# Experts' first layer as one fp32 matmul of 64 rows per tile, on alternating row halves of TensorE, in a MetaFormer block

## The reference, cut to what matters

```
xf = layernorm(t)                               # 2048 tokens x 64
logits = xf @ Wg + bg                           # 8 experts
top_w, top_i = top_k(logits, 2); top_w = softmax(top_w)
for e in range(8):                              # dense: every expert for every token
    h = gelu(xf @ W1[e] + b1[e])                # 64 -> 256, exact gelu
    out = out + w[:, e:e+1] * (h @ W2[e] + b2[e])   # 256 -> 64
t = t + out
```

## Time and profile before

| | |
|---|---|
| time of the profiled execution | 122.68 us |
| span from first to last instruction | 121.0 us |
| median of the three timed runs | 123.15 us |
| PE (matmul) busy | 116.2 us, 96% |
| DVE (VectorE) busy | 78.8 us, 65% |
| ACT (ScalarE) busy | 70.1 us, 58% |
| POOL (GpSimd) busy | 33.4 us, 28% |
| granted TensorE clock | 1.000 |

### The profile page before, as it was taken

The page is one execution under the profiler, slowest core; times in us unless marked ns, Lnnn a source line. Parts: engine busy times, 40 slices in busy tenths (PEclk is TensorE's granted clock), DMA queues, the critical chain, the costliest instruction groups (busy, mean ns, idle before and its releaser), DMA issues.

```text
span 121.0 us, 3332 instructions
## 1 busy us (share of the span) xinstructions
PE 116.2 (96%) x1282; PEld 86.3 (71%) x1282; DVE 78.8 (65%) x267; ACT 70.1 (58%) x134; POOL 33.4 (28%) x51
## 2 busy tenths in 40 slices
PE   6999999999999889999999999999999999999991
PEld 5589956777798688977766876766766667666660
DVE  0489595753868998988991089976409055096972
ACT  4338799030596255378892894591973929729200
POOL 6727999990000003033250031000000000000370
PEclk9999999999999999999999999999999999999999
DMA  3579600000000000000000059921099590001001
GB/s 105 176 169 215 176 8 0 5 5 5 0 0 5 0 3 0 0 5 0 0 0 3 11 158 232 240 69 43 11 242 225 197 241 11 0 0 54 1 0 46
DMA packets 5460, 8.05 MB, mean 67 GB/s; under 512 B 1412, under 2 KB 3908, under 8 KB 5444
## 3 DMA queue, kind: packets, MB, share of 16 engines
q1 hardware_dynamic: 5344, 7.80, 25.0%
q10 hardware_dynamic: 100, 0.03, 0.2%
HBM read 7.24 MB, written 0.59 MB: 65 GB/s over the span
## 4 chain that ended last, share of the span: by engine, by line
PE 83%; DVE 9%; ACT 2%; issue 2%; POOL 1%; POOLq 1%; DVEq 0%
PE PS L996 36%; PE PS L1293 18%; PE PS L1112 13%; PE PS L1071 2%; DVE HEADWISE L898 2%; PE PS L1178 2%; PE PS L1081 2%; PE PS L1008 2%; PE PS L1217 1%; PE PS L1094 1%; PE PS L1203 1%; POOL XP L449 1%; PE PS L1024 1%; DVE XB L717 1%; PE PS L1248 1%
## 5 line engine op out<-in xcount | busy, mean ns | idle before, releaser
L573 ACT ACTIVATE MS<-PS,B 128x512 f32<-128x512 f32 x48 | 29.1, 689 | 7.2 <-PE PS L996 7.0
L996 PE MATMUL PS<-XS,W1H 128*128 128x512 f32 x64 | 26.5, 414 | 0.0
L996 PE MATMUL PS<-XS,W1L 128*128 128x512 f32 x64 | 25.3, 395 | 0.0
L1293 PE MATMUL PS<-MS,W 128*64 128x256 f32 x192 | 22.3, 383 | 0.0
L874 DVE SCALAR_TENSOR_TENSOR WY<-PS,B,HEADWISE 128x256 f32<-128x256 f32 x24 | 10.5, 480 | 14.8 <-PE PS L1293 14.5
L1293 PEld LDWEIGHTS PS<-MS,W 128*64 128x64 f32 x192 | 13.2, 137 | 8.5 <-ACT MS L573 1.5
L1112 PE MATMUL PS<-HEADWISE,BANDS 32*32 32x448 f32 (+2 forms) x480 | 15.9, 564 | 0.0
L996 PEld LDWEIGHTS PS<-XS,W1H 128*128 128x128 f32 x64 | 12.0, 188 | 4.8 <-ACT MS L573 1.0
L449 POOL TENSOR_TENSOR XP<-XP,WY 128x256 f32<-128x256 f32 x4 | 3.2, 808 | 41.1 <-DVE WY L924 40.8
L1112 PEld LDWEIGHTS PS<-HEADWISE,BANDS 32*32 32x32 f32 x480 | 10.9, 103 | 4.5 <-issue 1.2
L996 PEld LDWEIGHTS PS<-XS,W1L 128*128 128x128 f32 x64 | 12.0, 188 | 1.8
(11 more groups left out here) (135 smaller groups left out, 182.6 us busy)
## 6 DMA issues: line engine op xcount, KB each, us to landing
HEADWISE<-spread_dram SPq DMA_DIRECT2D x14, 256.0 KB, 4.9
W<-in_w_dram SPq DMA_DIRECT2D x3, 512.0 KB, 7.9
X<-in_x_dram SPq DMA_DIRECT2D x2, 256.0 KB, 3.1
HEADWISE<-spread_dram SPq DMA_DIRECT2D x4, 128.0 KB, 3.1
out_dram<-XP SPq DMA_DIRECT2D x4, 128.0 KB, 2.6
W<-spread_dram SPq DMA_DIRECT2D x2, 256.0 KB, 5.3
VEC<-in_vectors_dram SPq DMA_DIRECT2D x1, 132.0 KB
WQ<-in_w_qkv_dram SPq DMA_DIRECT2D x2, 48.0 KB, 2.8
```

The costliest lines, as they stand in the source:

```text
L573: act.activation(hidden(n), PS[:, h_bank(n), :], ACT.Gelu, bias=B1[:, k:k + 1]).then_inc(gelu_done, 1)
L996: return pe.matmul(PS[0:parts, bank, cols[0]:cols[1]], lhsT, rhs, start=start, stop=stop)
L1293: i = pe.matmul(PS[C * b:C * b + C, bank, at:end], W2[:, KC * e + k, :], hidden(KC * (E * s + e) + k)[:, N * b:N * b + N], start=begins an ...
```

## The change

- W1 is used as it is, in fp32. `split_high` and `split_low`, `W1H`, `W1L` and `WGS` go; ScalarE only preloads the gelu table at that place.
- `scale` writes the same 64 normalised channels twice in one operation of 128 x 512; `low` goes. XS therefore holds the tokens twice, on rows 0 to 63 and on rows 64 to 127, as fp32.
- A hidden tile is one fp32 matmul over 64 rows: even tiles on the lower row half, odd tiles on the upper.
- The gate is one fp32 matmul over 64 rows per 128 tokens, with 8 columns; `read_gates` is one operation.
- `WH` has memory of its own, and its DMA and TensorE's first layers don't wait for the split.
- In the convolution the loops over r and c change places: r is the inner one, and all four `conv_ready` rise at the last four matmuls.

```diff
-        WGS = sb("WGS", [128, 2, E], F32R)
-        W1H, W1L = sb("W1H", [128, E * HID], F32R), sb("W1L", [128, E * HID], F32R)
+        WH = sb("WH", [128, KC, PT])
...
-            split_high()
+            act.preload_act_table(ACT.Gelu)
...
-            dve.wait_ge(w_high, 2)
-            split_low(0)
-            split_low(1)
-            dve.tensor_tensor(WGS[:, 1, :], WG[:, :], WGS[:, 0, :].bitcast(F32), ALU.subtract).then_inc(w_low, 1)
...
-                dve.tensor_tensor(XHL[:, s % 2, :, 0, :].bitcast(F32R), XC2[:, s % 2],
-                                  SM[:, s, 1, :].unsqueeze(2).broadcast_to([128, TILES, C]), ALU.mult).then_inc(hi_ready, 1)
-
-            def low(s):
-                dve.wait_ge(hi_ready, s + 1)
-                for t in range(TILES):
-                    i = dve.scalar_tensor_tensor(out=XHL[:, s % 2, t, 1, :].bitcast(F32R), in0=XC2[:, s % 2, t],
-                                                 scalar=SM[:, s, 1, t:t + 1], in1=XHL[:, s % 2, t, 0, :],
-                                                 op0=ALU.mult, op1=ALU.subtract)
-                i.then_inc(xh_ready, 1)
+                shape = [128, TILES, 2, C]
+                dve.tensor_tensor(XHL[:, s % 2], XC2[:, s % 2].unsqueeze(2).broadcast_to(shape),
+                                  SM[:, s, 1, :].unsqueeze(2).unsqueeze(2).broadcast_to(shape), ALU.mult).then_inc(xh_ready, 1)
...
                 for m in range(2, len(taps)):
-                    for r in range(4):
-                        for c in range(4):
+                    for c in range(4):
+                        for r in range(4):
                             i = tap(0, r, c, 2 - c // 2, c % 2, *taps[m], False, m == len(taps) - 1)
-                        if m == len(taps) - 1:
-                            i.then_inc(conv_ready, 1)
+                            if c == 3 and m == len(taps) - 1:
+                                i.then_inc(conv_ready, 1)
...
-                pe.wait_ge(w_low, 3)
+                pe.wait_ge(w1_in, 64)
...
-                        at = 2 * E * (TILES * (s - pairs[0]) + t)
-                        i = mm(GATE_BANKS[part], (at, at + 2 * E), XS[:, s, 128 * t:128 * t + 128],
-                               WGS[:, :, :].rearrange("p k e -> p (k e)"), True, True)
+                        at = E * (TILES * (s - pairs[0]) + t)
+                        i = mm(GATE_BANKS[part], (at, at + E), XS[0:C, s, 128 * t:128 * t + 128], WG[0:C, :], True, True)
...
-                    for m, w in enumerate((W1H, W1L)):
-                        i = mm(h_bank(n), (0, PT), w[:, 128 * k:128 * k + 128], XS[:, s, :], m == 0, m == 1)
-                    i.then_inc(h_ready, 1)
+                    rows = slice(C * (k % 2), C * (k % 2) + C)
+                    mm(h_bank(n), (0, PT), W1[rows, 128 * k:128 * k + 128], XS[rows, s, :], True, True).then_inc(h_ready, 1)
```

More of the change, by code:

```diff
@@ L20 @@
 F32 = mybir.dt.float32
-F32R = mybir.dt.float32r
 ALU = mybir.AluOpType
@@ L138, in build @@
         SM = sb("SM", [128, PAIRS, 2, TILES])
-        XS = sb("XS", [128, PAIRS, PT], F32R)
+        XS = sb("XS", [128, PAIRS, PT])
         PLACE = sb("PLACE", [128, 16, E], mybir.dt.uint32)
@@ L171, in hidden @@
                 else hidden_more[:, slot - IN_MS, :]
-        WH = W1[:, 0:2 * PT].rearrange("p (k t) -> p k t", k=2)
         outs = XP[:, :].rearrange("p (s n) -> p s n", s=PAIRS)
@@ L217, in build @@
         bn_guarded, inv_ready, wps_ready = sem("bn_guarded"), sem("inv_ready"), sem("wps_ready")
-        w_high, w_low = sem("w_high"), sem("w_low")
         ones_set, k_first, v_first = sem("ones_set"), sem("k_first"), sem("v_first")
@@ L222, in build @@
         v2_ready, r2_ready = sem("v2_ready"), sem("r2_ready")
-        xh_ready, hi_ready = sem("xh_ready"), sem("hi_ready")
+        xh_ready = sem("xh_ready")
         a_filled, a_read = ([sem(f"a_{k}{s}") for s in range(PAIRS)] for k in ("filled", "read"))
@@ L343, in spread_over_hidden @@
             def spread_over_hidden():
-                sp.wait_ge(w_low, 3)
                 for k in range(2):
@@ L489, in take_conv @@
                     act.activation(CV[:, n, r, :], PS[:, CONV_BANKS[n][r], :], ACT.Copy).then_inc(cv_s, 1)
[L491 to L495, removed]
             def first_k(s):
@@ L672, in take_conv @@
                     dve.tensor_copy(CV[:, n, r, :], PS[:, CONV_BANKS[n][r], :]).then_inc(cv_v, 1)
-            def split_low(part):
-                cols = slice(E * HID // 2 * part, E * HID // 2 * (part + 1))
-                dve.tensor_tensor(W1L[:, cols], W1[:, cols], W1H[:, cols].bitcast(F32), ALU.subtract).then_inc(w_low, 1)
             def first_v(s):
@@ L814, in read_gates @@
                 logits = LOGITS[:, tiles, :]
[L815 to L818, removed]
+                of = PS[:, GATE_BANKS[part], 0:E * count].rearrange("p (t e) -> p t e", e=E)
+                dve.tensor_tensor(logits, of, VEC[:, 4 * C:4 * C + E].unsqueeze(1).broadcast_to([128, count, E]), ALU.add)\
+                    .then_inc(gate_read, 1)
                 dve.wait_ge(gate_read, part + 1)
@@ L954, in _ @@
             scale(0)
-            low(0)
             centre(1)
@@ L962, in _ @@
             scale(1)
-            low(1)
             variance(2)
@@ L967, in _ @@
             scale(2)
-            low(2)
             read_gates(0)
@@ L974, in _ @@
             scale(3)
-            low(3)
             dve.wait_ge(b2_in, 32)
@@ L1122, in conv_vk @@
                 for m in (0, 1):
-                    for r in range(4):
-                        for c in (0, 1):
+                    for c in (0, 1):
+                        for r in range(4):
                             tap(0, r, c, 2, c, *taps[m], m == 0, False)
@@ L1127, in conv_vk @@
                 for m in (0, 1):
-                    for r in range(4):
-                        for c in (2, 3):
+                    for c in (2, 3):
+                        for r in range(4):
                             tap(0, r, c, 1, c - 2, *taps[m], m == 0, False)
                 for m in range(2, len(taps)):
-                    for r in range(4):
-                        for c in range(4):
+                    for c in range(4):
+                        for r in range(4):
                             i = tap(0, r, c, 2 - c // 2, c % 2, *taps[m], False, m == len(taps) - 1)
-                        if m == len(taps) - 1:
-                            i.then_inc(conv_ready, 1)
+                            if c == 3 and m == len(taps) - 1:
+                                i.then_inc(conv_ready, 1)
             def conv_q():
@@ L1141, in conv_q @@
                 for m, dy in enumerate(LINES):
-                    for r in range(4):
-                        for c in range(4):
+                    for c in range(4):
+                        for r in range(4):
                             i = tap(1, r, c, 0, c % 2, c // 2, dy, m == 0, m == DY - 1)
-                        if m == DY - 1:
-                            i.then_inc(conv_ready, 1)
+                            if c == 3 and m == DY - 1:
+                                i.then_inc(conv_ready, 1)
             pe.wait_ge(scaled_v, 4)
```

## The result

The changed kernel took 133.23 us as the median of five runs (131.51 to 133.68), the kernel before 123.18 (122.67 to 123.28): ratio 1.079, 95% interval 1.074 to 1.084. Slower, as forecast (130.8), but 0.4 us beyond the range (125.5 to 132.8). The profiled execution took 131.51 us, which is inside it. In four of the five executions TensorE's mean granted clock was 0.97 to 0.99 and the time 133.2 to 133.7 us; in the profiled one it was 1.000. That difference of 1.7 us had no term in my sum.

What follows compares the result with a forecast made beforehand. PE was taken to bound the kernel by rate, ACT beside it in bursts. Attention phase 2.5, second-gate burst 1.45 and five bursts 3.95 gave 7.9 on 121.0; with 1.7 outside the span 130.6, stated as 130.8 us, range 125.5 to 132.8.

Steps and rivals of the forecast that it cites:

- Pair of tiles: First layer on PE: two row halves run at once, 0.86 us a pair against 0.93 before, plus 0.11 fresh start.
- Bursts: Five bursts of eight hidden tiles: waits for gelu's banks make each 4.73 us instead of 3.94, 3.95 in all.
- Gates and attention phase: First layers and first gate during attention: gate +0.9 us, with waits for banks +2.5 us in all.
- Second-gate burst: Stretch with the second gate: second layers start 3.95 us later, of which 1.45 are new.
- the rival with free gates: Both gates: 64-row loads take half the time, so gates cost nothing extra, 129.0 us; chance 0.09.
- Convolution: New order of r and c in the convolution: 0, with ends -3.0 and +1.0 us.
- The rival: Convolution: it gains 3.0 us from the new order, the rest as forecast, 127.7 us; chance 0.13.
- Splits, `low`, dropped waits: Work taken from ACT and DVE before the first layer, and waits on the split: 0 each.
- Span: Whole profiled span: 121.0 us grows by 7.9 to 128.9, passed on whole to the end.

Runs made afterwards that it cites:

- one_half: The changed kernel with all hidden tiles on the lower row half: 155.79 and 156.01 us at clock 0.967, 167.8 and 168.0 at 0.897.
- short: The changed kernel with two experts of first layer in turn with two of second, from pair 1's fifth expert on: ratio 1.040, 127.65 to 130.28 us.
- gate_twice: The changed kernel with each gate matmul issued twice: 136.61 to 139.24 us, clock 0.962 to 0.986 in all six.

## Why the prediction was right in its mechanism and short in its sum

- **Pair of tiles.** 0.86 and 0.11 forecast, 0.97 measured; the halves overlap (one_half).
- **Bursts.** 4.73 forecast, 4.68 measured where the burst's first start is counted. From one second layer to the next the five bursts cost 0.96, 0.94, 0.75, 0.94 and, at the last operation on DVE (126.73 against 118.41), 0.73: 4.3 instead of 3.95. The three largest stand behind the turning of tokens, which is full-array work: there the first layer starts 0.31 after the turning (89.55 - 89.24), and before only 0.13. I had left out this switch:

```profile
84.28 0.38 PE L1248 MATMUL PS<-IDT,HEADWISE 128*128 128x128 f32 x2
84.41 0.48 PE L996 MATMUL PS<-XS,W1H 128*128 128x512 f32 x1
```
- **Gates and attention phase.** 2.5 forecast, 2.5 measured, made of 2.8 less 0.2 for the convolution. Second-gate burst 1.45 forecast, 1.5 measured (4.0 - 2.5). Gate matmuls 0.11 apart, as taken from the nearest row; the rival with free gates fell.
- **Convolution.** 0 forecast with ends -3.0 and +1.0; -0.2 in this profile, -0.6 where it was tried alone. The rival had the sign but not the size: that matmuls share a row group with their neighbours is at most 0.6 of the missing 4 us.
- **Splits, `low`, dropped waits.** 0, and nothing in the chain answers to them.
- **Span.** 7.9 forecast, 8.3 to the last operation on DVE, 8.8 in the span; the last 0.5 is the store of the output, which took 2.6 us from issue to the end (127.19 to 129.8) instead of 2.1 and which I can't explain.
- **The step that failed** is one I did not write: the sum "121.0 + 7.9", plus the time outside the span, was taken to be passed on at a granted clock of 1.000, as in the kernel before: a term put at nothing without a reason. I had foreseen the 1.8 us of gate and the waits around it, and I did not ask what TensorE's clock would do there. In four of the five measured executions a lower clock cost 1.7 us or a little more; for the three at 0.987 that is 3.4 us at half speed, by the short profile behind the first gate. With it the forecast would have been 132.3 to 132.5. The other 0.9 between forecast and profile (130.6 against 131.51) is the bursts and the end of the span, as above.
- **How sure that is.** That the executions at 133.2 to 133.7 us had the low mean clock is measured. That a gate can bring it is shown by gate_twice (6 of 6 executions, the first fall inside the gate); in the changed kernel itself no dip was seen in a profile, its place is taken from short, and one_half had none at its first gate. What stays open is why the share was 4 of 5 in one set and 1 of 10 in the two others. That the median fell outside the range hung on this share: the ten executions at full clock took 130.93 to 131.54 and once 132.72, all inside.

## What to carry to other kernels

Cutting the matmuls of a tile by running two tiles at once makes their results come together and later; where another engine empties a ring of banks one by one, count when the first result is ready and when the last bank is free, for bursts as well as for rates. A saving by rate of 0.07 us a pair was here worth less than one fresh start (0.11 to 0.2). And where an edit lengthens a stretch in which TensorE does little but load weights, allow for a stretch at half clock at or behind it (1.7 us here, in a third of the executions). Cutting that stretch up and putting it into waits that are there anyway gave 1.2 us at full clock; whether it also keeps the clock up is not shown.

## What I had not expected of the hardware

- In the profile of short TensorE's clock fell to 0.5 for 3.4 us though PE was busy 100% of the time before it, with 16 loads of 128 columns with 8 columns of matmul each and then tiles on half the array. The executions of one kernel differ in it: 5 of 15 of the changed one had a low mean clock.
- In one_half, where the first layer uses only half of the array, the clock was 0.967 or 0.897 in all four; the same gates stand in it.
- The store of 128 KB at the end took 2.1 us in one profile and 2.6 in another.
